# Expert stage of a convolution, attention and mixture-of-experts kernel: expert groups issued interleaved with four weight slots, output written two images at a time

## Chip, cores and metric

The kernel runs on one core of a Trainium2 chip (trn2). The metric is the device time of one execution in microseconds (us), lower is better. A comparison is made over several runs, by their median.

## What is computed

The input is four images of 128 channels by 64 by 64 pixels. Layer 0 adds a deformable 3x3 convolution, layer 1 adds an attention block and then a layer of 64 experts with top-8 routing over the tokens of each image. The change touches the last of these only, which the reference writes so (x is the token tensor, 4 x 4096 x 128, after a layer norm):

```
logits = jnp.einsum('bsd,ed->bse', x, gate_w) + gate_b
probs = jax.nn.softmax(logits, axis=1)
vals, idx = jax.lax.top_k(probs.transpose(0, 2, 1), K)
...
pooled = jnp.einsum('bked,bke->bed', gathered, topv)
h = jax.nn.gelu(jnp.einsum('ebd,edh->ebh', h, weight1), approximate=False)
out = jnp.einsum('ebh,eho->ebo', h, weight2)
weighted = jnp.einsum('beo,bke->bkeo', out, topv).reshape(Bn, K * E, O)
outputs = outputs.at[jnp.arange(Bn)[:, None], flat_idx].add(weighted)
```

The result is `t + outputs`, turned back to channels by pixels. Biases stand as an extra row of `weight1` and `weight2`. All of it is f32.

## The kernel before, in words

The program is a chain of stages with a barrier between them: offsets, first convolution, the main stage (attention with the convolution and the feed-forward of other images beside it), a last feed-forward round, and `stage_experts`. The first four are the same on both sides. All instructions are written out by hand for each engine, and the order on an engine is the order of the code; semaphores tie the engines together.

`stage_experts` has three parts, in this order:

- **Routing**, two images at a time (a duo). Tokens are loaded to `xn`, normalised on ACT, turned on PE by transposes (L1640), multiplied with the gate (L1650); DVE picks the top 8 and makes `sel[duo]`, a 128 x 4096 matrix whose rows 0 to 63 are the experts of the duo's first image and rows 64 to 127 those of its second. `sel` is turned (L1656) and pools the tokens (L1665) into `pooled`.
- **Experts**, 16 groups of four. For a group, `weights` on SP (L1504, L1506) issues five DMAs, 2 MB in all, into one of `SLOTS` = 2 slots, as soon as the product that read the slot before is done (`o_full`). PE multiplies the four experts' pooled vectors (4 columns each, put at column tiles 0, 32, 64, 96) with the first weights (L1679, `eps_h`), ACT copies the result (L1625), PE turns it (L1683), DVE adds the bias (L1571), ACT applies Gelu (L1627), PE does 16 products with the second weights (L1688, `eps_o`), DVE copies (L1573), PE turns it (L1692), DVE adds the second bias (L1576). Only then does PE start the next group: nothing of group g+1 overlaps group g but its weights' loading. The code is a loop whose body has two groups.
- **Output**, 32 steps, one chunk of 512 tokens of one image each. PE makes the chunk's expert sum, a product over the 64 rows of that image in `sel` (L1704), and adds the tokens themselves by four products of a token tile with the identity into the same PSUM bank (L1706). DVE copies the bank to `y` (L1584), SP stores it (L1491). Two banks and two `y` buffers alternate. The tokens are loaded again from memory, 2 MB an image, the first two images after all weights, the others during the output (L1519).

Of the kernel before, what the change touches and what calls it, by code (L numbers as in the profile page):

```python
# [10 lines left out]
ALU = mybir.AluOpType  # L11
# [3 lines left out]
P = 128  # L15
# [1425 lines left out]
SLOTS = 2  # L1441


def stage_experts(nc, d, ident, stack):
# [18 lines left out]
    pooled, pooled_g = sb("pooled", [P, NEXP, IMAGES]), [sb(f"pooled_g{i}", [P, EXPERTS_AT_ONCE, IMAGES]) for i in range(SLOTS)]  # L1463

    hs = [sb(f"hs{i}", [P, 512]) for i in range(SLOTS)]
    hb = [sb(f"hb{i}", [P, 4, EXPERTS_AT_ONCE, IMAGES]) for i in range(SLOTS)]
    hg = [sb(f"hg{i}", [P, 4, EXPERTS_AT_ONCE, IMAGES]) for i in range(SLOTS)]
    os = [sb(f"os{i}", [P, P]) for i in range(SLOTS)]
    out_t, out_e = sb("out_t", [P, IMAGES, NEXP]), [sb(f"out_e{i}", [P, P]) for i in range(DUOS)]
    y = [sb(f"y{i}", [P, 512]) for i in range(2)]  # L1470
# [3 lines left out]
     dv, bias_full, bias_done, pg_ready, h_full, hs_ready, ht_full, hb_ready, hg_ready, o_full, os_ready, ot_full, o_done, oe_full,  # L1474
     oe_done, y_full, y_free, cleared, ln_ready) = (
        sem(n) for n in ("e_consts", "e_biases", "e_tr_full", "e_tr_free", "lg_full", "lg_free", "xn_ready", "ex_ready", "s_ready",
                         "st_full", "pool_full", "pool_free", "top_ready", "e_dve", "bias_full", "bias_done", "pg_ready", "h_full",
                         "hs_ready", "ht_full", "hb_ready", "hg_ready", "o_full", "os_ready", "ot_full", "o_done", "oe_full",
                         "oe_done", "y_full", "y_free", "e_cleared", "ln_ready"))
    x_in = [sem(f"e_x_in{i}") for i in range(2)]  # L1480
    w_in = [sem(f"w_in{i}") for i in range(SLOTS)]
    y_out = [sem(f"y_out{i}") for i in range(2)]
# [4 lines left out]

    def stores(sp, b):
        for c in range(CHUNKS):
            sp.wait_ge(y_free, b * CHUNKS + c + 1)  # L1490
            sp.dma_start(d.out[b, :, c * 512:(c + 1) * 512], y[c % 2][:]).then_inc(y_out[c % 2], 16)  # L1491

    @block.sync
    def _(sp):
# [18 lines left out]
        with sp.Fori(1, NG // SLOTS) as i:  # L1513
            for s in range(SLOTS):
                sp.wait_ge(o_full, (i - 1) * SLOTS + s + 1)
                weights(i * SLOTS + s, s)
        for b in range(IMAGES):
            sp.wait_ge(pool_full, IMAGES) if b < 2 else sp.wait_ge(y_full, (b - 1) * CHUNKS)
            sp.dma_start(xn[b % 2][:], tokens(b)).then_inc(x_in[b % 2], 16)  # L1519
            if b:  # L1520
                stores(sp, b - 1)
        stores(sp, IMAGES - 1)
        for i in range(2):
            sp.wait_ge(y_out[i], IMAGES * CHUNKS // 2 * 16)

    @block.vector
    def _(dve):
# [36 lines left out]
        with dve.Fori(0, NG // SLOTS) as i:  # L1564
            for s in range(SLOTS):
                g = i * SLOTS + s
                es = bass.ds(g * EXPERTS_AT_ONCE, EXPERTS_AT_ONCE)
                v.tensor_copy(pooled_g[s][:], pooled[:, es, :]).then_inc(pg_ready, 1)
                dve.wait_ge(ht_full, g + 1)
                bias1 = b1_t[:, :, es].rearrange("p c (e o) -> p c e o", o=1).to_broadcast([P, 4, EXPERTS_AT_ONCE, IMAGES])  # L1570
                v.tensor_tensor(hb[s][:], ps_t[0][:].rearrange("p (c e b) -> p c e b", c=4, b=32)[:, :, :, 0:IMAGES], bias1, ALU.add).then_inc(hb_ready, 1)  # L1571
                dve.wait_ge(o_full, g + 1)
                v.tensor_copy(os[s][:], ps_o[:, 0:P]).then_inc(os_ready, 1)  # L1573
                dve.wait_ge(ot_full, g + 1)
                bias2 = b2_t[:, es].rearrange("p (o e) -> p o e", o=1).to_broadcast([P, IMAGES, EXPERTS_AT_ONCE])
                v.tensor_tensor(out_t[:, :, es], ps_t[1][:, 0:P].rearrange("p (e b) -> p b e", b=32)[:, 0:IMAGES, :], bias2, ALU.add).then_inc(o_done, 1)  # L1576
# [3 lines left out]
        for n in range(IMAGES * CHUNKS):  # L1580
            dve.wait_ge(y_full, n + 1)
            if n >= 2:
                dve.wait_ge(y_out[n % 2], n // 2 * 16)
# [248 lines left out]
```

## Time and profile before

| | |
|---|---|
| median of 3 runs | 8955.63 us (8911.77, 8955.63, 8959.74) |
| profiled execution: its own time | 8972.61 us |
| profiled execution: span of the trace | 8970.8 us |
| PE, ACT, DVE, POOL busy | 7595.3, 7673.2, 3781.7, 1154.8 us |
| mean granted TensorE clock | 0.936 |
| expert groups (8714.4 to 8838.1) | 123.7 us |
| output steps (8839.2 to 8967.5) | 128.3 us |

The trace is of one execution. Times in it are counted from the start of the span. PE is the matrix engine (PEld its weight loads), ACT, DVE, POOL and SP are the other engines; SPq rows are DMAs that SP issues. A granted clock of 1.00 is 2.4 GHz, 0.50 is 1.2 GHz. A product of f32 operands shows as two records of PE, a transpose as one. "DMA share" is the mean busy share of the core's 16 DMA engines; since it counts the time of packets that overlap in an engine, it can be somewhat over 1.

### The profile page before, as it was taken

The numbers are of one execution on the slowest core, as the hardware profiler recorded it, in microseconds if no ns is written. First come the engines' busy times: TensorE is split into PE (matmuls) and PEld (weight loads), VectorE is DVE, ScalarE is ACT, GpSimd is POOL, SyncE is SP. The second block draws the span as 40 slices with busy tenths as digits, with TensorE's granted clock in tenths as the row PEclk, the third lists the DMA queues.
The fourth block names the chain that finished last, engine by engine and source line by source line (L and its number), as shares of the span: only waits on it lengthen the run. The fifth ranks groups of instructions, "written<-read, shape, count | busy, mean of one in ns | idle before, by whom it ended". The sixth has DMA issues, their size and how long they took to land. (4 is left out here: it accounts for less than half of the span.)

```text
span 8970.8 us, 172356 instructions
## 1 busy us (share of the span) xinstructions
PE 7595.3 (85%) x59323; PEld 2167.8 (24%) x59323; DVE 3781.7 (42%) x14439; ACT 7673.2 (86%) x6204; POOL 1154.8 (13%) x1165
## 2 busy tenths in 40 slices
PE   4354989999999999999999999999988888888558
PEld 1343222222222222222222222222222121212134
DVE  4566333333334555454555454544533222224421
ACT  1222999999999999999999999999999999998541
POOL 0553111111111111111111111111000000000000
PEclk8676999999999999999999999999999999999775
DMA  6553111111111111111111111111100000000115
GB/s 211 165 150 99 49 48 50 47 49 48 49 48 49 51 50 50 48 52 52 51 50 50 49 52 45 50 53 51 31 11 7 8 8 8 7 8 13 52 49 176
DMA packets 514912, 491.53 MB, mean 55 GB/s; under 512 B 228057, under 2 KB 417177, under 8 KB 513570
## 3 DMA queue, kind: packets, MB, share of 16 engines
q0 software_dynamic: 92880, 304.42, 11.7%
q1 hardware_dynamic: 421202, 176.26, 7.5%
q8 instruction: 494, 8.09, 0.4%
q14 instruction: 336, 2.75, 0.1%
HBM read 398.77 MB, written 81.79 MB: 54 GB/s over the span
## 5 line engine op out<-in xcount | busy, mean ns | idle before, releaser
L921 ACT ACTIVATE e<-sc 128x1536 f32<-128x1536 f32 x5376 | 7281.0, 1678 | 182.8 <-PE sc L852 176.6
L871 PE MATMUL acc<-e,v_cur 128*9 128x512 f32 x32256 | 4333.9, 602 | 9.8 <-DVE acc_sb L803 9.8
L852 PE MATMUL sc<-b_unit,a_cur 32*128 32x512 f16 x16384 | 2184.2, 388 | 627.6 <-ACT e L921 567.8
L852 PEld LDWEIGHTS sc<-b_unit,a_cur 32*128 32x128 f16 x16384 | 538.7, 91 | 4560.6 <-ACT e L921 4148.9
L553 POOL DMA_INDIRECT corners<-table,idx_st x873 | 867.6, 994 | 4754.8 <-ACT e L921 4657.9
L871 PEld LDWEIGHTS acc<-e,v_cur 128*9 128x9 f32 x32256 | 485.9, 88 | 965.2 <-issue 953.8
L577 DVE SCALAR_TENSOR_TENSOR val<-corners,w_st,val 128x128 f32<-128x128 f32 x2619 | 711.5, 346 | 1.8
L803 DVE COPY acc_sb<-acc 128x512 f32<-128x512 f32 x129 | 89.2, 692 | 1371.5 <-PE acc L871 1350.4
L500 PE MATMUL cf_ps_t<-ident,cf_val 128*128 128x128 f32 x1152 | 172.9, 311 | 271.4 <-DVE cf_val L421 154.0
L475 ACT COPY cf_val_t<-cf_ps_t 128x512 f32<-128x512 f32 (+1 forms) x96 | 44.0, 479 | 404.1 <-PE cf_ps_t L500 266.8
L382 POOL DMA_INDIRECT cf_corners<-table,cf_idx x288 | 287.0, 997 | 473.3 <-DVE cf_idx L407 236.1
L591 DVE COPY val_t<-misc 128x512 f32<-128x512 f32 (+1 forms) x288 | 160.8, 558 | 433.4 <-PE misc L624 432.3
L632 PE MATMUL misc<-dcnw,val_t 128*128 128x128 f32 x1728 | 243.8, 286 | 0.0
L500 PEld LDWEIGHTS cf_ps_t<-ident,cf_val 128*128 128x128 f32 x1152 | 163.0, 225 | 279.6 <-issue 278.3
L632 PEld LDWEIGHTS misc<-dcnw,val_t 128*128 128x128 f32 x1728 | 207.3, 191 | 43.5 <-issue 43.5
L814 DVE RECIPROCAL rs<-misc 128x16 f32<-128x16 f32 x129 | 33.1, 256 | 392.4 <-PE misc L825 392.0
L754 DVE COPY a_next<-misc 128x1024 f16<-128x1024 f16 (+1 forms) x64 | 44.3, 692 | 354.4 <-PE misc L766 349.0
L600 DVE TENSOR_TENSOR t_out<-misc,xt 128x128 f32<-128x128 f32 x96 | 28.0, 292 | 379.6 <-PE misc L632 379.6
L575 DVE TENSOR_SCALAR val<-corners,w_st 128x128 f32<-128x128 f32 x873 | 180.1, 282 | 12.4 <-DVE ctx_t L816 12.1
L421 DVE SCALAR_TENSOR_TENSOR cf_val<-cf_corners,cf_w,cf_val 128x128 f32<-128x128 f32 x576 | 157.5, 346 | 43.4 <-remote 35.5
L921 ACT ACTIVATE e_tail<-sc 128x1024 f32<-128x1024 f32 x128 | 173.6, 1356 | 0.0
L1017 DVE TENSOR_SCALAR val_t<-misc 128x512 f32<-128x512 f32 x96 | 66.4, 692 | 254.1 <-PE misc L1052 254.1
(326 smaller groups left out, 4854.9 us busy)
## 6 DMA issues: line engine op xcount, KB each, us to landing
table<-pix SPq DMA_DIRECT2D x16, 2304.0 KB, 18.4
ew<-in_ew SPq DMA_DIRECT2D x16, 1024.0 KB, 5.4
ew<-in_ew SPq DMA_DIRECT2D x64, 256.0 KB, 6.1
corners<-table,idx_st POOLq DMA_INDIRECT x873
x_ch<-in_x SPq DMA_DIRECT2D x4, 2048.0 KB, 10.8
qn<-q SPq DMA_DIRECT2D x64, 128.0 KB
ctx<-ctx_t SPq DMA_DIRECT2D x128, 64.0 KB, 1.8
out<-y SPq DMA_DIRECT2D x32, 256.0 KB, 2.0
```

Of the source, the lines that this page charges most:

```text
L382: pool.indirect_dma_start(corners[j][:, k, :], None, d.table, bass.IndirectOffsetOnAxis(idx_st[j][:, k:k + 1], 0)).then_inc(gathered[j], 16)
L421: last = v.scalar_tensor_tensor(out=dst, in0=src, scalar=wt, in1=dst, op0=ALU.mult, op1=ALU.add)
L500: last = nc.tensor.matmul(ps_t[at % 2][:, (k - g0) * P:(k - g0 + 1) * P], val[j % 2][c][:, k, :], r.ident[:], start=(c == 0), stop=(c == 1))
L553: pool.indirect_dma_start(self.corners[s][:, k, :], None, self.d.table, bass.IndirectOffsetOnAxis(self.idx_st[s][:, k:k + 1], 0)).then_inc ...
L575: last = v.tensor_scalar(val[:, k, :], src, wt, None, ALU.mult)
L577: last = v.scalar_tensor_tensor(out=val[:, k, :], in0=src, scalar=wt, in1=val[:, k, :], op0=ALU.mult, op1=ALU.add)
L591: m.dve_give(v.tensor_copy(self.val_t[:, g0 * P:g1 * P], m.bank[:, 0:(g1 - g0) * P]))
L632: last = self.nc.tensor.matmul(m.bank[:, 0:P], self.val_t[:, k * P:(k + 1) * P], self.r.dcnw[:, k, :], start=(k == 0), stop=(k == TAPS - 1))
L803: self.nc.vector.tensor_copy(self.acc_sb[:], self.acc[:]).then_inc(self.acc_read, 1)
L852: last = self.nc.tensor.matmul(self.sc[k % self.SC][:, i, :], self.a[rows, t * P:(t + 1) * P], self.bst[u % 2][rows, :], start=True, stop= ...
L871: last = self.nc.tensor.matmul(self.acc[32 * h:32 * h + self.E1, :], self.v[:, t, h, :], self.e_of(j)[:, i, :], start=(t == 0), stop=(t == ...
L921: self.nc.scalar.activation(self.e_of(j)[:], self.sc[k % self.SC][:, 0:width, :], ACT.Exp, scale=1.0 / HD ** 0.5).then_inc(self.exp_done, 1)
```

## The change

- **Four weight slots** in place of two; the slots of `hs`, `hb`, `hg`, `os` stay two. `pooled_g`, a copy of four experts' columns, goes away, and PE reads `pooled` itself.
- **Groups are interleaved.** The loops are written out. PE's order for step g is: turn of the hidden values of g, hidden product of g+1, turn of the outcome of g-1, outcome product of g. DVE takes over the copy of the hidden product from ACT (`copy_h`), so ACT does only Gelu.
- **The tokens are loaded again between the weights**: image 0 before the weights of group 4, then one image before those of groups 7, 10 and 13, into four places (`raw`) that are free by then. After the last weights SP has only stores left.
- **Output in 16 steps of two images.** Each step handles the same chunk of both images of a duo: two products over 64 rows each (rows 0 to 63 and rows 64 to 127) into two banks (`sums`), then eight transposes of token tiles into two further banks (`turns`). ACT copies the turned tokens to `y`, which now lies in `xn_t`, DVE adds the sum from PSUM in place, SP stores two pieces of 256 KB.

```diff
-SLOTS = 2
+SLOTS = 4
...
-    y = [sb(f"y{i}", [P, 512]) for i in range(2)]
+    y = [[xn_t[:, (2 * j + i) * 512:(2 * j + i + 1) * 512] for i in range(2)] for j in range(2)]
...
+    raw = [xn[0][:], xn[1][:], big[:].rearrange("p (t c) -> p t c", c=P), s_t[:]]
+    sums = ((ps_l[0], ps_l[1]), (ps_h, ps_o))
+    turns = ((ps_t[0], ps_t[1]), (ps_p, ps_b))
...
+        sp.wait_ge(pool_full, IMAGES)
+        sp.wait_ge(s_ready, DUOS)
+        for g in range(SLOTS, NG):
+            if (g - SLOTS) % 3 == 0:
+                b = (g - SLOTS) // 3
+                sp.dma_start(raw[b], tokens(b)).then_inc(again[b], 16)
+            sp.wait_ge(o_full, g - SLOTS + 1)
+            weights(g, g % SLOTS)
+        for step in range(STEPS_OUT):
+            duo, c = divmod(step, CHUNKS)
+            for i in range(2):
+                sp.wait_ge(y_free, 2 * step + i + 1)
+                sp.dma_start(d.out[2 * duo + i, :, c * 512:(c + 1) * 512], y[c % 2][i]).then_inc(y_out[c % 2][i], 16)
...
+        copy_h(0)
+        for g in range(NG):
+            add_b1(g)
+            if g + 1 < NG:
+                copy_h(g + 1)
+            if g:
+                add_b2(g - 1)
+            copy_o(g)
+        add_b2(NG - 1)
...
+        for step in range(STEPS_OUT):
+            at = step % 2
+            dve.wait_ge(y_full, step + 1)
+            for i in range(2):
+                dve.wait_ge(turned, 2 * step + i + 1)
+                v.tensor_tensor(y[at][i], y[at][i], sums[at][i][:], ALU.add).then_inc(y_free, 1)
...
+        for step in range(STEPS_OUT):
+            at = step % 2
+            act.wait_ge(y_full, step + 1)
+            for i in range(2):
+                if step >= 2:
+                    act.wait_ge(y_out[at][i], step // 2 * 16)
+                nc.scalar.copy(y[at][i], turns[at][i][:]).then_inc(turned, 1)
...
+        hidden(0)
+        for g in range(NG):
+            turn_hidden(g)
+            if g + 1 < NG:
+                hidden(g + 1)
+            if g:
+                turn_outcome(g - 1)
+            outcome(g)
+        turn_outcome(NG - 1)
...
-                T.matmul(ps_l[c % 2][:], out_e[b // 2][half, :], sel[b // 2][half, c * 512:(c + 1) * 512], start=True, stop=False)
+            if step >= 2:
+                pe.wait_ge(y_free, 2 * (step - 1))
+            for i in range(2):
+                half = slice(NEXP * i, NEXP * (i + 1))
+                T.matmul(sums[at][i][:], out_e[duo][half, :], sel[duo][half, c * 512:(c + 1) * 512], start=True, stop=True)
+            for i in range(2):
                 for j in range(4):
-                    last = T.matmul(ps_l[c % 2][:, j * P:(j + 1) * P], xn[b % 2][:, 4 * c + j, :], ident[:], start=False, stop=(j == 3))
+                    last = T.transpose(turns[at][i][:, j * P:(j + 1) * P], raw[2 * duo + i][:, 4 * c + j, :], ident[:])
+            last.then_inc(y_full, 1)
```

The order of PE in the expert part. The engine is PE, the place is the loop body before (two groups; `eps_h` is the hidden product, `eps_t<-ident,hs` its turn, `eps_o` the outcome, `eps_t<-ident,os` its turn):

```order
L1679 MATMUL eps_h<-ew_0,pooled_g 4x512 [waits hs_ready,pg_ready]
L1679 MATMUL eps_h<-ew_0,pooled_g 4x512 x3
L1683 MATMUL eps_t<-ident,hs 128x128 [waits hs_ready]
L1683 MATMUL eps_t<-ident,hs 128x128 x3
L1688 MATMUL eps_o<-ew_0,hg 4x128 [waits hg_ready]
L1688 MATMUL eps_o<-ew_0,hg 4x128 x15
L1692 MATMUL eps_t<-ident,os 128x128 [waits o_done,os_ready]
L1676 REGISTER_ALU [waits w_in1]
L1679 MATMUL eps_h<-ew_1,pooled_g 4x512 [waits hs_ready,pg_ready]
```

and the same engine in the change, at the last groups:

```order
L1711 MATMUL eps_h<-ew_3,pooled 4x512 [waits w_in3]
L1711 MATMUL eps_h<-ew_3,pooled 4x512 x3
L1732 MATMUL eps_t<-ident,os 128x128 [waits o_done,os_ready]
L1726 MATMUL eps_o<-ew_2,hg 4x128 [waits hg_ready]
L1726 MATMUL eps_o<-ew_2,hg 4x128 x15
L1718 MATMUL eps_t<-ident,hs 128x128 [waits hb_ready,hs_ready]
L1718 MATMUL eps_t<-ident,hs 128x128 x3
L1732 MATMUL eps_t<-ident,os 128x128 [waits o_done,os_ready]
L1726 MATMUL eps_o<-ew_3,hg 4x128 [waits hg_ready]
L1726 MATMUL eps_o<-ew_3,hg 4x128 x15
L1732 MATMUL eps_t<-ident,os 128x128 [waits o_done,os_ready]
```

The hidden product of group 15 (slot 3), which waits for the last weights, now stands ahead of the outcome of group 14.

The queue of DMAs that SP issues, in the change, from the end of routing (before, the loads of tokens `xn_tok<-t` stood behind the last `ew`):

```order
L1518 DMA xn_tok<-t 128x32x128 [waits s_ready,pool_full]
L1504 DMA ew_0<-in_ew 128x4x512 [waits o_full]
L1506 DMA ew_0<-in_ew 128x4x128 x4
L1504 DMA ew_1<-in_ew 128x4x512 [waits o_full]
L1506 DMA ew_1<-in_ew 128x4x128 x4
L1504 DMA ew_2<-in_ew 128x4x512 [waits o_full]
L1506 DMA ew_2<-in_ew 128x4x128 x4
L1518 DMA xn_tok<-t 128x32x128
L1504 DMA ew_3<-in_ew 128x4x512 [waits o_full]
```

The tokens of image 0 moved ahead of the weights of group 4, and those of image 1 ahead of group 7's.

PE in the output, before:

```order
L1704 MATMUL eps_l<-selected,out_e 128x512 [waits y_free]
L1706 MATMUL eps_l<-ident,xn_tok 128x128 x4
L1704 MATMUL eps_l<-selected,out_e 128x512 [waits y_free]
L1706 MATMUL eps_l<-ident,xn_tok 128x128 x4
L1704 MATMUL eps_l<-selected,out_e 128x512 [waits y_free]
```

and now:

```order
L1757 MATMUL eps_l<-selected,out_e 128x512 [waits e_again1,e_again0,oe_done]
L1757 MATMUL eps_l<-selected,out_e 128x512
L1760 MATMUL eps_t<-ident,xn_tok 128x128 x8
L1757 MATMUL eps_h<-selected,out_e 128x512
L1757 MATMUL eps_o<-selected,out_e 128x512
L1760 MATMUL eps_p<-ident,xn_tok 128x128 x4
L1760 MATMUL eps_b<-ident,xn_tok 128x128 x4
L1757 MATMUL eps_l<-selected,out_e 128x512 [waits y_free]
```

Two products stand next to each other where one stood, and the eight token tiles are transposes (one record each) where they were products (two records each).

## Rows read from the trace of the kernel before

**Rows 1.** The page, busy time by engine.

```profile
PE 7595.3 (85%) x59323; PEld 2167.8 (24%) x59323; DVE 3781.7 (42%) x14439; ACT 7673.2 (86%) x6204; POOL 1154.8 (13%) x1165
```

**Rows 2.** Stretches: length, busy PE, PEld, DVE, ACT, POOL; clock, DMA share, GB/s.

```profile
8714.40:8838.10 123.70, 82.78 (x720) 32.08 (x720) 13.69 (x64) 32.71 (x47) 0.00 (x0) 0.54 0.91 259
8839.20:8967.50 128.30, 128.26 (x320) 72.90 (x320) 21.44 (x31) 0.00 (x0) 0.00 (x0) 0.50 0.32 106
```

**Rows 3.** Timeline of one expert group: start, us, engine, line, operation.

```profile
8752.69 1.89 PE L1679 MATMUL eps_h<-ew,pooled_g 128*4 128x512 f32 x8 [0.51 <-DVE pooled_g L1568]
8754.65 0.58 ACT L1625 COPY hs<-eps_h 128x512 f32<-128x512 f32 x1 [5.30 <-PE eps_h L1679]
...
8755.29 1.11 PE L1683 MATMUL eps_t<-ident,hs 128*128 128x128 f32 x4 [0.71 <-ACT hs L1625]
...
8757.10 1.89 PE L1688 MATMUL eps_o<-ew,hg 128*4 128x128 f32 x32 [0.69 <-ACT hg L1627]
...
8759.40 0.48 PE L1692 MATMUL eps_t<-ident,os 128*128 128x128 f32 x1 [0.41 <-DVE os L1573]
...
8760.01 0.18 DVE L1576 TENSOR_TENSOR out_t<-eps_t,b_t 128x16 f32 x1 [0.67 <-PE eps_t L1692]
```

**Rows 4.** Timeline of SP's queue: first reload of weights, reload of tokens.

```profile
8720.24 0.38 SPq L1504 DMA_DIRECT2D ew<-in_ew  x1
...
8824.87 8.92 SPq L1519 DMA_DIRECT2D xn_tok<-t  x2
```

**Rows 5.** Stretches, columns as in rows 2: the transfers.

```profile
8736.00:8826.00 90.00, 60.84 (x506) 22.98 (x507) 9.75 (x46) 24.47 (x35) 0.00 (x0) 0.52 0.94 269
8490.00:8510.00 20.00, 0.00 (x0) 0.00 (x0) 11.23 (x79) 0.27 (x1) 0.00 (x0) 0.50 1.05 298
...
8850.00:8860.00 10.00, 10.00 (x28) 6.09 (x27) 2.00 (x3) 0.00 (x0) 0.00 (x0) 0.50 0.13 52
```

**Rows 6.** Timeline: the last group's first product, the first of the output.

```profile
8830.62 1.89 PE L1679 MATMUL eps_h<-ew,pooled_g 128*4 128x512 f32 x8 [0.52 <-DVE pooled_g L1568]
...
8839.24 2.07 PE L1704 MATMUL eps_l<-selected,out_e 64*128 64x512 f32 x2 [0.38 <-DVE out_e L1579]
```

**Rows 7.** Groups of the output by shape: operation, count, busy, mean ns, idle before.

```profile
L1706 PE MATMUL eps_l<-ident,xn_tok 128*128 128x128 f32 x256 | 66.4, 441 | 0.0
L1704 PE MATMUL eps_l<-selected,out_e 64*128 64x512 f32 x64 | 66.3, 1138 | 0.4 <-DVE out_e L1579 0.4
...
L1584 DVE COPY y<-eps_l 128x512 f32<-128x512 f32 x32 | 22.1, 692 | 106.9 <-PE eps_l L1706 102.4 <-DMA out<-y 4.6
```

**Rows 8.** Timeline of output steps.

```profile
8849.25 2.07 PE L1706 MATMUL eps_l<-ident,xn_tok 128*128 128x128 f32 x8
8851.26 2.07 PE L1704 MATMUL eps_l<-selected,out_e 64*128 64x512 f32 x2
```

**Rows 9.** Products over 32 rows in the main stage: the page's group.

```profile
L852 PE MATMUL sc<-b_unit,a_cur 32*128 32x512 f16 x16384 | 2184.2, 388 | 627.6 <-ACT e L921 567.8
```

**Rows 10.** Timeline of the main stage: three of them together.

```profile
4000.66 0.39 PE L852 MATMUL sc<-b_unit,a_cur 32*128 32x512 f16 x3
```

**Rows 11.** Transposes of the routing: timeline, and durations min/median/max in ns.

```profile
8522.20 6.15 PE L1640 MATMUL eps_t<-ident,xn_tok 128*128 128x128 f32 x32 [46.47 <-ACT xn_tok L1593]
```

```profile
L1640 PE MATMUL eps_t<-ident,xn_tok x128: 272/273/477, 8522.2 to 8663.3; 128*128 128x128 f32 x128
```

**Rows 12.** Stretches, columns as in rows 2: where those transposes run, and output steps.

```profile
8521.90:8525.30 3.40, 3.10 (x14) 2.74 (x15) 0.00 (x0) 1.57 (x4) 0.00 (x0) 0.50 0.00 0
8525.30:8528.70 3.40, 3.21 (x21) 2.02 (x20) 0.00 (x0) 3.07 (x6) 0.00 (x0) 1.00 0.00 0
8840.00:8900.00 60.00, 60.00 (x151) 34.17 (x150) 10.24 (x15) 0.00 (x0) 0.00 (x0) 0.50 0.35 114
```

**Rows 13.** The end: last copy, and the stores' time to landing.

```profile
8967.56 0.69 DVE L1584 COPY y<-eps_l 128x512 f32<-128x512 f32 x1 [3.31 <-PE eps_l L1706]
```

```profile
DMA to landing us min/median/max: 2.0/2.0/8.4
```

More of the change, by code:

```diff
@@ L1512, in _ @@
             sp.dma_start(xn[b % 2][:], tokens(b)).then_inc(x_in[b % 2], 16)
[L1513 to L1524, printed above, removed]
+        sp.wait_ge(pool_full, IMAGES)
[11 more added lines that the diff above has]
+                sp.dma_start(d.out[2 * duo + i, :, c * 512:(c + 1) * 512], y[c % 2][i]).then_inc(y_out[c % 2][i], 16)
+        for j in range(2):
+            for i in range(2):
+                sp.wait_ge(y_out[j][i], STEPS_OUT // 2 * 16)
     @block.vector
@@ L1563, in _, with copy_h @@
         dve.wait_ge(bias_done, 2)
[L1564 to L1576, printed above, removed]
+        def copy_h(g):
+            dve.wait_ge(h_full, g + 1)
+            if g >= 2:
+                dve.wait_ge(ht_full, g - 1)
+            v.tensor_copy(hs[g % 2][:], ps_h[:]).then_inc(hs_ready, 1)
@@ new lines, in hidden, with turn_hidden @@
+        def hidden(g):
+            s = g % SLOTS
+            pe.wait_ge(w_in[s], (g // SLOTS + 1) * 16 * (1 + EXPERTS_AT_ONCE))
+            for e in range(EXPERTS_AT_ONCE):
+                last = T.matmul(ps_h[32 * e:32 * e + IMAGES, :], pooled[:, g * EXPERTS_AT_ONCE + e, :], w1[s][:, e, :], start=True, stop=True)
+            last.then_inc(h_full, 1)
+        def turn_hidden(g):
+            pe.wait_ge(hs_ready, g + 1)
+            pe.wait_ge(hb_ready, g)
+            for c in range(4):
+                last = T.transpose(ps_t[0][:, c * P:(c + 1) * P], hs[g % 2][:, c * P:(c + 1) * P], ident[:])
+            last.then_inc(ht_full, 1)
@@ new lines, in outcome, with turn_outcome @@
+        def outcome(g):
+            s = g % SLOTS
+            pe.wait_ge(hg_ready, g + 1)
+            for c in range(4):
+                for e in range(EXPERTS_AT_ONCE):
+                    last = T.matmul(ps_o[32 * e:32 * e + IMAGES, 0:P], hg[g % 2][:, c, e, :], w2[s][:, e, c, :], start=(c == 0), stop=(c == 3))
+            last.then_inc(o_full, 1)
+        def turn_outcome(g):
+            pe.wait_ge(os_ready, g + 1)
+            pe.wait_ge(o_done, g)
+            T.transpose(ps_t[1][:, 0:P], os[g % 2][:], ident[:]).then_inc(ot_full, 1)
```

94 lines of the change are left out of this document (41 added, 53 removed).

## Prediction

> **What bounds the kernel now.** I read the page's busy times first, then the stretches of the expert stage, then timelines inside them. PE and ACT are busy for 85% and 86% of the span [rows 1], but that is the main stage, which the change leaves alone. What counts is the last 256 us, where the stretches show two parts [rows 2]. In the expert groups (123.7 us for 16, so 7.7 us each) PE is busy for 82.8 us only, and the DMA engines at a share of 0.91. In the output (128.3 us for 32 steps) PE is busy all the time, at a granted clock of 0.50, which is 1.2 GHz, with DMA at 0.32. So the output is bound by PE at its low clock. The groups are bound twice, closely: by a serial chain and, nearly, by the transfers.
>
> The chain is seen in one group's timeline [rows 3]: product 1.89, copy on ACT 0.58, turn 1.11, then 0.7 us for bias and Gelu (8756.40 to 8757.10), product 1.89, copy and turn, second bias done at 8760.19. PE works 1.89 + 1.11 + 1.89 + 0.48 = 5.4 us of it. The transfers: in the middle of the part, 269 GB/s at a share of 0.94 [rows 5].
>
> **The expert groups after the change.** Interleaved, a group costs PE at least 5.4 us at the low clock, 86 us for 16 groups. But what is transferred between the end of routing (about 8713) and the last group grows. Before, 14 groups of weights (2.097 MB each) were loaded there, from 8720.24 on, and the tokens only from 8824.87 [rows 4]. Now 12 groups and four images of tokens, also 2.097 MB each, are: 16 units, 33.6 MB. At a full share the rate is 269 / 0.94 = 286 GB/s; the deeper queue at the start of the stage gives 298 / 1.05 = 284 [rows 5]. So 117.5 us. The first packets can move at about 8714.5, since the tokens of image 0 are issued as soon as pooling is done, and the weights of group 4 are queued behind them when group 0 frees its slot, so there is no hole. The last weights land at about 8832; before, the last group's product started at 8830.62 [rows 6].
>
> Behind the last weights now stands more than before: hidden product of group 15 (1.9), then, since it was put ahead of them, turn 13 (0.5) and the outcome of 14 (1.9), then turn 15 (1.1), bias and Gelu (0.7), outcome 15 (1.9) and its copy, turn and bias (1.2, 8758.99 to 8760.19) [rows 3]; with 0.5 for the landing about 10 us. The part ends at 8842 where it ended at 8838.1: **+4 us**. The overlap is paid for by the tokens; it does not shorten the part. Bounds: the highest rate seen, 298 GB/s, gives 113 us, thus -1; the mean rate of the whole part before, 259 [rows 2], gives 130 us, thus +16. The stretch at the start of the stage is nearest, since it too has several transfers queued.
>
> Small edits of this part cost nothing: `pooled_g` goes (0.2 us per group, off the path now); the copy on DVE takes 0.69 in place of 0.58 [rows 7, 3] and lies under the outcome product of 1.89. If the transfers were faster than PE, that copy would still be hidden. Loading four slots at the start adds 4.2 MB, 15 us of transfers, early in the stage, when nothing else is loaded before image 2.
>
> **The output, one step.** Before, a step is 128.3 / 32 = 4.0 us: from the token products to the sum's product 2.0 us, and 2.0 us back [rows 2, 8]. In the change a step covers two chunks. Its eight transposes are eight records, as the four token products were: 2.0 us (four take 1.11 us with the last one's run-out [rows 3]). Its two sum products use rows 0 to 63 and rows 64 to 127 of the array. What they cost together no row shows for this shape. From below: as one, 2.0 us. From above: one after the other, 4.0 us. The nearest rows are products over 32 rows, each 388 ns long, of which three end 0.39 us after the first began, so they run side by side [rows 9, 10]; and for f32 the four hidden products on different columns, eight records, take 1.89 us, where two records alone take 2.07 [rows 3, 8]. I take 2.0. A step is then 4.0 us at the low clock, for twice the work: 16 steps, 64 us.
>
> **The clock.** Here I go one step on. All through the output the clock is 0.50 though PE is busy for 60.00 of 60 us [rows 12], and half of that time is a product that uses only 64 of the 128 rows [rows 7]. At the first transposes of the routing, over all 128 rows, 3.10 of 3.40 us busy, the clock was at 0.50 too, and after those 3.4 us it was at 1.00 and stayed there [rows 12]. These were transposes alone [rows 11]. In the changed output both halves of the rows are at work together, then transposes over all of them, so nothing is left that uses half of the array. I expect the clock to rise in the first steps and stay up. The Trainium skill ("TensorE: Matmul & The Clock Gate", Part 4: PE-mode transpose) says the opposite of transposes: the full clock does not engage for them. By it the sum would be -59 us rather than -86; this trace does not agree with it [rows 11, 12].
>
> At the full clock PE's half of a step halves, to 2.0 us. Then the chain counts: PE's last run-out 0.2, two copies on ACT of 0.58, one add on DVE of 0.69 behind the second, and three hand-overs, together 2.3 us, before PE may use the same banks. Two steps then take 2.0 + 2.3 = 4.3, thus 2.2 us each. DVE (1.4) and ACT (1.2) fit. Two stores a step are 524 KB in 2.2 us, 240 GB/s; a stretch of stores alone moved 52 GB/s at a share of 0.13, thus 400 at full share [rows 5], and a store lands 2.0 us after issue [rows 13], before ACT wants its buffer two steps on. With 5 us at the low clock first (1.25 steps): 5 + 14.75 x 2.2 = 37.5 us, against 128.3: **-91 us**. Bounds: 34 (2.0 a step) and 64 (low clock). If the store becomes late, ACT is next, at some 3 us a step.
>
> **The end.** Before, one copy on DVE (0.69) and a store follow the last product [rows 13]; now two copies on ACT and the add: **+1 us**.
>
> **Sum:** +4 - 91 + 1 = -86 us, against the profiled execution's own 8972.61 (span 8970.8), thus 8887. That execution is 17 us above the median of the runs, 8955.63, so I predict 8955.6 - 86 = 8870 us.
>
> **Rivals.** All against the median.
> - *The clock stays low.* For it: 128 us of busy PE at 0.50 [rows 2]. Against it: the rise after transposes [rows 12]. The output takes 64 us: +4 - 64 + 1 = -59, thus 8897. The page of the Trainium skill named above would have it so.
> - *The two sum products run one after the other.* They are f32 products of two records each, and no row shows such a pair on different rows. A step is then 6 us, and since half the rows idle again, the clock stays low: 96 us, +4 - 32 + 1 = -27, thus 8929.
> - *ACT, DVE and the stores set the pace* at 3 us a step: 5 + 14.75 x 3 = 49 us, +4 - 79 + 1 = -74, thus 8882.
> - *Slower than before: the transfers choke.* Tokens and weights in one long queue, with the last weights behind all of it. It decides once the rate falls below 33.6 MB / (117.5 + 86) = 165 GB/s. At 150 GB/s the transfers take 224 us in place of 117.5: +4 + 106 - 91 + 1 = +20, thus 8976; over 0.5% slower needs some 135 GB/s. Against it: 298 GB/s with as many transfers queued [rows 5].
> - *The overlap does nothing* is not a rival but part of the forecast.
>
> **How the numbers follow.** The forecast has a chance of 0.62, the low clock 0.16, the pair in turn 0.11, the pace of the copies 0.08, the choked transfers 0.03. The runs of one kernel lie between 8912 and 8960, and one profile at 8973, so the level itself may move. The range goes from the forecast on the lowest of those levels, 8912 - 86 = 8826, to the low clock on the highest, 8897 + 17 = 8914, rounded to 8825 and 8915; it leaves out the pair in turn and the choke, 0.14. About 0.5%, 45 us, is what a measurement can tell from no change. Over it lie the forecast, the low clock and the pace of the copies, 0.86, less a little since 59 is close to 45: faster 0.84. Same 0.13, slower 0.03.
>
> **What would show it.** Expert groups: DMA share near 1 from 8714 on, PE waiting for `ew` from about group 7 on, the part ending within a few us of 8842. Output: the pair of sum products as four records in 2.1 us or less, not 4; 16 steps; clock 1.00 from the second or third step; steps of 2.0 to 2.3 us; ACT's waits on `out<-y` small. Wrong if the clock stays at 0.50, if the sum products stand in a row, or if the last weights land after 8845.

## The result and the profile after

| | before | after |
|---|---|---|
| median (4 runs each, taken together) | 8948.38 us (8911.77 to 8959.74) | 8840.6 us (8838.6 to 8852.54) |
| ratio, 95% interval | | 0.989 [0.9873, 0.9906] |
| profiled execution: own time, span | 8972.61, 8970.8 | 8852.54, 8850.7 |
| end of routing (last copy of `pooled`) | 8713.3 | 8696.7 |
| expert part, from there to the last `out_t` | 124.8 | 113.4 |
| gap to the first sum product | 1.1 | 1.0 |
| output, from there to the end of the span | 131.5 | 39.7 |
| **from the end of routing to the end** | 257.5 | 154.1 |

The forecast was 8870 in a range of 8825 to 8915; the median is 8840.6. The spans differ by 120.1 us. Of that, 16.6 lie ahead of the end of routing. They lie ahead of the expert stage too: its first load is issued at 8487.1 before and at 8469.7 after, and from there to the end of routing it is 226.2 and 227.0 us, so the two more slots that are loaded there cost less than 1 us. Over the 13 profiled kernels of this study the end of routing lies anywhere from 8673 to 8718, which is variation between executions. The change itself is the last line, **-103.4 us**, where the forecast's sum was -86. All experiments are judged by that line. It comes from one execution of each kernel, but parts that two kernels have in common agree closely in it: the expert part of after, e2, e3 and e7 takes 113.4 to 113.6 us, the output of after, e5, e6, e8 and e9 39.6 to 39.9. The medians stand beside it; they carry the variation ahead of the stage.

The page of after, busy time by engine, beside [rows 1]:

```profile
PE 7470.6 (84%) x59195; PEld 2103.8 (24%) x59195; DVE 3787.0 (43%) x14439; ACT 7662.5 (87%) x6205; POOL 1126.8 (13%) x1165
```

PE loses 125 us of busy time, more than the span does. The stretches of after: the expert part, the output, the output's inner steps, and the middle of the expert part (length, busy PE, PEld, DVE, ACT, POOL; clock, DMA share, GB/s), beside [rows 2, 5]:

```profile
8696.40:8810.10 113.70, 61.69 (x725) 26.93 (x725) 21.57 (x67) 4.10 (x16) 0.00 (x0) 0.74 1.02 296
8810.10:8850.70 40.60, 34.30 (x194) 18.74 (x194) 21.05 (x34) 17.36 (x32) 0.00 (x0) 0.99 0.56 207
8811.00:8846.00 35.00, 33.74 (x192) 18.54 (x192) 19.24 (x31) 16.29 (x30) 0.00 (x0) 1.00 0.57 210
8706.00:8800.00 94.00, 46.33 (x499) 19.08 (x495) 14.18 (x44) 2.82 (x11) 0.00 (x0) 0.70 1.11 323
```

Three things are to be seen. The output runs at a clock of 1.00 where it ran at 0.50. PE is busy for only 54% of the expert part, so something else sets its length. And the DMA engines move 323 GB/s at a share of 1.11, while the forecast took 286 GB/s, the rate at a share of 1.00, for full.

The output in detail, from the timeline of after (start, us, engine, line, operation), beside [rows 8]:

```profile
8819.50 1.13 PE L1757 MATMUL eps_l<-selected,out_e 64*128 64x512 f32 x4
8819.56 0.58 ACT L1661 COPY xn_ch<-eps_p 128x512 f32<-128x512 f32 x1 [1.01 <-PE eps_b L1760]
...
8820.24 0.69 DVE L1612 TENSOR_TENSOR xn_ch<-xn_ch,eps_h 128x512 f32<-128x512 f32 x1 [0.80 <-ACT xn_ch L1661]
8820.56 1.09 PE L1760 MATMUL eps_t<-ident,xn_tok 128*128 128x128 f32 x8
...
8821.59 0.69 PE L1757 MATMUL eps_h<-selected,out_e 64*128 64x512 f32 x1
...
8821.59 0.69 PE L1757 MATMUL eps_o<-selected,out_e 64*128 64x512 f32 x1
...
8823.72 1.13 PE L1757 MATMUL eps_l<-selected,out_e 64*128 64x512 f32 x4
```

Two records of different banks (`eps_h`, `eps_o`) begin at the same time and take 0.69 us: the pair on rows 0 to 63 and 64 to 127 does run side by side. All four records of a pair take 1.13 us. Two steps take 8823.72 - 8819.50 = 4.22 us, 2.11 each.

What the expert part waits for, from the waits of 8700 to 8851 (engine, line, what it waited for: us in total, times, longest):

```profile
ACT hg L1654 <- DVE hb L1581: 121.5, 16, 18.0
...
PE eps_h L1711 <- DMA ew<-in_ew: 49.3, 12, 9.2
...
DVE xn_ch L1612 <- ACT xn_ch L1661: 16.6, 16, 2.9
```

ACT's 121.5 us are those of an engine with nothing else to do. PE waits for weights at each of the 12 loaded groups, 49.3 us in all: the part is bound by transfers. The last group, beside [rows 6]:

```profile
8804.61 1.04 PE L1711 MATMUL eps_h<-ew,pooled 128*4 128x512 f32 x8 [1.66 <-DMA ew<-in_ew]
...
8809.92 0.17 DVE L1593 TENSOR_TENSOR out_t<-eps_t,b_t 128x16 f32<-128x16 f32 x1 [0.42 <-PE eps_t L1732]
...
8811.07 1.13 PE L1757 MATMUL eps_l<-selected,out_e 64*128 64x512 f32 x4 [0.47 <-DVE out_e L1606]
```

The hidden product took 1.04 us, at the full clock, where it took 1.89 before [rows 6]; and the tail behind the last weights is 8810.1 - 8804.6 = 5.5 us. The granted clock is 1.00 from 8802.38 on, so the output inherits it from the last expert groups. How they came to raise it is not isolated by any run. It is not the length of the part: with two slots (e5, below) the part is 195.7 us long, and the output starts at 1.00 all the same.

### The profile page after: what moved, and what is told of

The parts are those of the page before. It is cut to its first block and busy times, and to the rows that moved or that the text cites. A ratio compares the mean times of both kernels' runs of the same rounds, so it can differ in the third digit from the quotient of the medians.

```text
span 8850.7 us, 171835 instructions
## 1 busy us (share of the span) xinstructions
PE 7470.6 (84%) x59195; PEld 2103.8 (24%) x59195; DVE 3787.0 (43%) x14439; ACT 7662.5 (87%) x6205; POOL 1126.8 (13%) x1165
## 5 line engine op out<-in xcount | busy, mean ns | idle before, releaser
L553 POOL DMA_INDIRECT corners<-table,idx_st x873 | 839.9, 962 | 4778.7 <-ACT e L921 4682.0
L803 DVE COPY acc_sb<-acc 128x512 f32<-128x512 f32 x129 | 89.2, 692 | 1369.8 <-PE acc L871 1350.3
L575 DVE TENSOR_SCALAR val<-corners,w_st 128x128 f32<-128x128 f32 x873 | 179.9, 281 | 12.5 <-DVE ctx_t L816 12.5
```

The lines of the kernel that those rows point to most:

```text
L553: pool.indirect_dma_start(self.corners[s][:, k, :], None, self.d.table, bass.IndirectOffsetOnAxis(self.idx_st[s][:, k:k + 1], 0)).then_inc ...
L575: last = v.tensor_scalar(val[:, k, :], src, wt, None, ALU.mult)
L803: self.nc.vector.tensor_copy(self.acc_sb[:], self.acc[:]).then_inc(self.acc_read, 1)
```

## The experiments

Edits are against the changed kernel unless said. In the table, part, output and total are the stretches of the table above in one profiled execution (the total has the gap between part and output in it); the median and ratio are against the kernel before, measured beside it.

| run | what differs | part | output | total | median | ratio, 95% |
|---|---|---|---|---|---|---|
| before | | 124.8 | 131.5 | 257.5 | 8948 to 8958 | |
| after | | 113.4 | 39.7 | 154.1 | 8840.6 | 0.989 [0.9873, 0.9906] |
| e1_out_only | groups of before, output of after | 121.2 | 51.0 | 179.5 | 8858.6 | 0.9907 [0.9887, 0.9927] |
| e2_groups_only | groups of after, output of before | 113.5 | 130.3 | 244.7 | 8935.0 | 0.9973 [0.9954, 0.9992] |
| e3_split_pair | the pair taken apart | 113.4 | 100.7 | 215.1 | 8897.8 | 0.9942 [0.9925, 0.9958] |
| e4_full_rows | before, sum product over 128 rows | 125.6 | 80.2 | 207.7 | 8883.6 | 0.9924 [0.9905, 0.9943] |
| e5_two_slots | two slots | 195.7 | 39.6 | 236.3 | 8934.1 | 0.9975 [0.9958, 0.9992] |
| e6_in_series | four slots, groups in series | 116.6 | 39.7 | 157.3 | 8867.0 | 0.9888 [0.9859, 0.9916] |
| e7_by_products | products in place of transposes | 113.6 | 53.3 | 167.9 | 8864.4 | 0.9894 [0.9877, 0.991] |
| e8_long_rows | second weights in 2 KB pieces | 104.3 | 39.6 | 144.9 | 8832.5 | 0.9861 [0.9843, 0.9879] |
| e9_three_slots | three slots | 125.8 | 39.9 | 166.7 | 8866.5 | 0.9895 [0.9861, 0.9929] |
| e10_late_tokens | two images' tokens after the weights | 101.3 | 41.6 | 143.8 | 8850.3 | 0.9882 [0.9853, 0.9911] |
| e11_long_late | e8 and e10 together | 89.2 | 40.3 | 130.5 | 8821.6 | 0.9857 [0.9828, 0.9885] |

### Which half does it, and what raises the clock

**e1_out_only** takes the groups back to the order and the two slots of before, with the copy of the hidden product on ACT again, and puts all tokens after the weights. The loops stay written out, and PE reads `pooled` itself.

```diff
-SLOTS = 4
+SLOTS = 2
...
-            if (g - SLOTS) % 3 == 0:
-                b = (g - SLOTS) // 3
-                sp.dma_start(raw[b], tokens(b)).then_inc(again[b], 16)
             sp.wait_ge(o_full, g - SLOTS + 1)
             weights(g, g % SLOTS)
+        for b in range(IMAGES):
+            sp.dma_start(raw[b], tokens(b)).then_inc(again[b], 16)
...
         for g in range(NG):
+            hidden(g)
             turn_hidden(g)
-            if g + 1 < NG:
-                hidden(g + 1)
-            if g:
-                turn_outcome(g - 1)
             outcome(g)
+            turn_outcome(g)
```

> The new output with the groups as they were before (in series, two slots, tokens loaded after the last weights). Theory A, two images at once put all 128 rows to work and that raises the clock: the output starts at 0.50, as the groups end at 0.50, and goes to 1.00 within 5 us; the 16 steps take 37 us, the kernel about 90 us less than before, 8858. Theory B, the clock was high in the changed kernel only because the groups handed it over high: it stays at 0.50, the 16 steps take 64 us, the kernel 63 less than before, 8885.

**e2_groups_only** is the other half: 32 output steps of one image, as before.

```diff
-                T.matmul(sums[at][i][:], out_e[duo][half, :], sel[duo][half, c * 512:(c + 1) * 512], start=True, stop=True)
+                T.matmul(ps_l[c % 2][:], out_e[b // 2][half, :], sel[b // 2][half, c * 512:(c + 1) * 512], start=True, stop=False)
...
-                    last = T.transpose(turns[at][i][:, j * P:(j + 1) * P], raw[2 * duo + i][:, 4 * c + j, :], ident[:])
+                    last = T.matmul(ps_l[c % 2][:, j * P:(j + 1) * P], raw[b][:, 4 * c + j, :], ident[:], start=False, stop=(j == 3))
```

> The new groups, slots and loads with the output as it was before (32 steps, products over 64 rows, tokens by products with the identity). The groups take 114 us, 11 less than before, in either theory, and hand over the clock at 1.00. Theory A with a strict reading (half the rows idle lets the clock fall): the output is back at 0.50 and 128 us, the kernel 11 under before, 8937. Theory B, the clock once up stays up under a busy PE: 32 steps at 2.05 us, 66 us, the kernel 73 under before, 8875.

**e3_split_pair** keeps everything but the pair: each sum product is followed by its own four transposes.

```diff
                 T.matmul(sums[at][i][:], out_e[duo][half, :], sel[duo][half, c * 512:(c + 1) * 512], start=True, stop=True)
-            for i in range(2):
                 for j in range(4):
```

> The changed kernel with the two sum products of a step pulled apart: product and four transposes of one image, then of the other. If the pair runs side by side in the changed kernel, a step gets longer by one product at the full clock, 0.9 to 1.1 us: 16 steps take 50 us in place of 35, the kernel 8856. If standing together is worth nothing: no change, 8841. If half-used rows also lose the clock: 96 us for the steps, 8902.

**e4_full_rows** is the kernel before with one edit: `out_e` has a tile for each image whose other 64 rows are zero, and the sum product goes over all 128 rows.

```diff
-                T.matmul(ps_l[c % 2][:], out_e[b // 2][half, :], sel[b // 2][half, c * 512:(c + 1) * 512], start=True, stop=False)
+                T.matmul(ps_l[c % 2][:], out_e[b][:], sel[b // 2][:, c * 512:(c + 1) * 512], start=True, stop=False)
```

> The kernel before, with one edit: the sum product of each image runs over all 128 rows, the expert values of the other image's 64 rows set to zero, so PE does as many steps of the same length on the same order. Theory A: the clock rises within 5 us of the output's start and stays, the 32 steps take about 70 us in place of 128, the kernel 58 under before, 8890. Theory B: nothing in the output itself raises it, it stays at 0.50, no change, 8948.

Stretches of e1: the wait ahead of the output with its first product, the output's first steps, the next ones:

```profile
8794.20:8801.20 7.00, 0.55 (x2) 0.15 (x2) 0.51 (x2) 0.00 (x0) 0.00 (x0) 0.50 1.06 290
8801.20:8805.70 4.50, 4.45 (x14) 2.60 (x16) 0.00 (x0) 0.44 (x1) 0.00 (x0) 0.50 1.06 291
8805.80:8815.90 10.10, 6.01 (x36) 3.18 (x32) 2.57 (x4) 1.61 (x4) 0.00 (x0) 1.00 1.05 304
```

Here the rise can be seen that the forecast spoke of: the output begins at 0.50, and after 4.5 us of pairs and transposes the clock is 1.00. Stretches of e2, at the first products and then to the end:

```profile
8807.60:8810.00 2.40, 2.39 (x9) 1.64 (x10) 0.00 (x0) 0.00 (x0) 0.00 (x0) 0.80 0.03 7
8810.00:8934.00 124.00, 124.00 (x311) 70.42 (x310) 21.44 (x31) 0.00 (x0) 0.00 (x0) 0.50 0.17 66
```

The expert groups handed over a full clock, and in this execution the steps of before lost it within 2 us and did not have it again, with PE busy for every one of 124 us. Splitting the pair does the same (e3, output), and filling the rows undoes it (e4, its first steps, and the steps up to a stall):

```profile
8807.50:8898.00 90.50, 90.49 (x181) 36.31 (x182) 18.00 (x28) 15.48 (x29) 0.00 (x0) 0.51 0.22 82
```

```profile
8808.40:8813.80 5.40, 5.33 (x13) 3.27 (x14) 0.71 (x2) 0.00 (x0) 0.00 (x0) 0.50 0.76 207
8813.90:8837.70 23.80, 18.49 (x109) 13.52 (x107) 6.23 (x9) 0.00 (x0) 0.00 (x0) 1.00 0.59 198
```

e4 adds no useful work, only zeros on the idle half of the rows, and takes 51 us off the output. So what holds the clock down in these profiled executions is the product over 64 of 128 rows when it is alone, and what raises it is all rows at work, be it by a pair or by zeros. In e3, one image's half step takes 3.05 us (the timeline of its PE):

```profile
8851.74 2.07 PE L1757 MATMUL eps_o<-selected,out_e 64*128 64x512 f32 x2
8853.75 1.11 PE L1759 MATMUL eps_b<-ident,xn_tok 128*128 128x128 f32 x4
8854.79 2.07 PE L1757 MATMUL eps_l<-selected,out_e 64*128 64x512 f32 x2
```

That is 6.1 us for two images, the 6 us of the rival "the pair in turn"; its output of 100.7 us is that rival's 96 and its end. The two halves of the change, from 257.5: the output alone gives -78.0, the groups alone -12.8, together they give -103.4. The 12.6 us between come from e1's end: its gap and output are 17.5 us longer than those of after (51.0 + 7.2 against 39.7 + 1.0), of which 4.8 are covered, since its part is 3.6 shorter than that of before and the output of e2 1.2 shorter. PE waits for tokens first, and then stores stand in the queue behind the tokens of images 2 and 3. The waits of e1:

```profile
ACT xn_ch L1659 <- DMA out<-xn_ch: 10.7, 3, 8.4
...
PE eps_l L1751 <- DMA xn_tok<-t: 6.5, 1, 6.5
```

In e4, whose tokens of images 2 and 3 are loaded during the output too, the same thing costs more (DVE's waits):

```profile
DVE y L1587 <- DMA out<-y: 18.8, 3, 8.3
```

Two of e2's ten runs took 8876.1 and 8890.1 at a mean clock of 0.947 and 0.946, where its profiled run had 0.940. The faster one is at what the expectation gives for a clock that stays up through the whole output (8875). The level ahead of the stage does not explain it: with e2's 244.7 us behind it, the end of routing would lie at 8630, 43 us earlier than in any of the 13 profiles. So it seems that a full clock, once handed over, can also be kept by steps with half-filled rows. Neither execution was profiled; this is an inference, and what decides between the two courses is open.

**e7_by_products** takes the transposes away and keeps the pair.

```diff
-                    last = T.transpose(turns[at][i][:, j * P:(j + 1) * P], raw[2 * duo + i][:, 4 * c + j, :], ident[:])
+                    last = T.matmul(turns[at][i][:, j * P:(j + 1) * P], raw[2 * duo + i][:, 4 * c + j, :], ident[:], start=True, stop=True)
```

> The changed kernel with the tokens turned by f32 products with the identity (two records each) in place of transposes (one each). If PE sets the step: 8 records more at 0.11 us at the full clock, 0.9 us a step, 14 us in all, 8855. If the copies on ACT and DVE set it: no change, 8841. The clock stays at 1.00 in either case.

Its output, and its eight token products in the timeline:

```profile
8810.40:8856.00 45.60, 45.59 (x300) 32.43 (x300) 18.00 (x28) 15.03 (x28) 0.00 (x0) 1.00 0.42 156
```

```profile
8817.56 2.05 PE L1760 MATMUL eps_t<-ident,xn_tok 128*128 128x128 f32 x16
```

PE is busy all the time, at 1.00: 16 records take 2.05 us where 8 transposes took 1.09. The output is longer by 13.6 us for 16 steps, 0.85 each; the transposes give that and nothing else. The clock is full with them and without them. The Trainium skill ("TensorE: Matmul & The Clock Gate", Part 4: PE-mode transpose) has it, from another kernel, that transposes do not engage the full clock. Here transposes alone went from 0.50 to 1.00 [rows 11, 12], and in after, steps of which half are transposes keep 1.00 for 35 us, so the measurement decides against that sentence here.

### What shortens the expert part

**e6_in_series** keeps the four slots and the tokens between the weights, but runs group after group, on PE as shown and on DVE in the same way.

```diff
         for g in range(NG):
+            hidden(g)
             turn_hidden(g)
-            if g + 1 < NG:
-                hidden(g + 1)
-            if g:
-                turn_outcome(g - 1)
             outcome(g)
+            turn_outcome(g)
```

> The changed kernel with four slots and tokens between the weights, but each group after the other on PE as before. Theory A, the interleaving is what lets the part follow the transfers: PE's series of 7.7 us a group decides, the part takes 125 us in place of 114 and hands the clock over low, which costs the output 2 to 3 us: 8855. Theory B, the transfers decide in either order and only the last group is slower, by 2 us: 8843.

**e5_two_slots** and **e9_three_slots** keep the interleaved order and change the number of slots (`SLOTS = 2`, `SLOTS = 3`), with one condition more so that still just four images of tokens are loaded.

> The changed kernel with two weight slots in place of four, interleaved groups and tokens between the weights kept; 14 groups of weights and 4 images are then loaded in the part, 18 units in place of 16. Theory A, the rate of 317 GB/s comes of the deeper queue that four slots allow: it falls to about 280, the part takes 135 + 8 = 143 us in place of 114, the kernel 8870. Theory B, the rate belongs to the mix of transfers and the written-out code: 317 stays, the part takes 119 + 8 = 127 us, the kernel 8854.

> The changed kernel with three weight slots, interleaved groups and tokens between the weights kept; 13 groups and 4 images in the part, 17 units. From the end of pooling to the end of the kernel the changed kernel takes 154.1 us. Theory A, the stall of two slots comes of the order (the load into a slot waits for a product that stands behind the next group's weights), and three slots leave two loads outstanding, enough to keep the DMA engines full: 35.7 MB at 320 GB/s, the part 120 us in place of 113.4, 161 in all, the kernel 8848. Theory B, the rate grows with the queue's depth and three slots give 285 GB/s: the part 133 us, 174 in all, 8861.

The middle of e6's part, and its waits for weights:

```profile
8712.00:8810.00 98.00, 56.96 (x594) 22.94 (x594) 18.17 (x53) 3.33 (x13) 0.00 (x0) 0.67 1.10 320
```

```profile
PE eps_h L1707 <- DMA ew<-in_ew: 17.2, 4, 8.6
```

With the groups in series the DMA engines still move 320 GB/s, and PE still waits for weights; the part is 3.2 us longer, 116.6, which is what the theory that transfers decide gives (116; the chain theory gave 125). So with four slots **interleaving is worth 3 us**. The rest is there without it: e6 is 8.2 us below the part of before, although 16 units of 2.097 MB (12 groups and four images) are loaded in it where 14 were. Of these 8.2 us, 3.6 come with e1 already (121.2), which has two slots and the groups in series as well; what is left to explain them are the written-out loops and PE's reading of `pooled` itself. Against e1, e6 has the two slots more, the tokens in between and the copy on DVE, and needs 4.6 us less for two units more. The median of e6, 8867.0, lies over both theories (8843 and 8855) and does not decide between them; the part and the total (157.3) do. With two slots it is the other way round, and neither theory had foreseen the size. The timeline of e5, two groups:

```profile
8740.27 0.37 SPq L1504 DMA_DIRECT2D ew<-in_ew  x1
...
8748.98 1.89 PE L1711 MATMUL eps_h<-ew,pooled 128*4 128x512 f32 x8 [7.73 <-DMA ew<-in_ew]
...
8751.21 1.51 PE L1726 MATMUL eps_o<-ew,hg 128*4 128x128 f32 x32
8752.79 0.37 SPq L1504 DMA_DIRECT2D ew<-in_ew  x1
...
8761.52 1.89 PE L1711 MATMUL eps_h<-ew,pooled 128*4 128x512 f32 x8 [8.21 <-DMA ew<-in_ew]
```

In the interleaved order the outcome of g stands behind the hidden product of g+1. The slot of g is free only after that outcome, and g+1 has the other slot: when the load for g+2 is issued, the one for g+1 has just been used, and no other weights are on their way. Each load of weights runs by itself, 8.7 us from issue (8740.27) to use (8748.98), then 3.8 us of PE work, and again: 12.5 us a group. PE waits for weights 14 times, 117.5 us in all, and the part moves 193 GB/s on average. More slots are not a bonus to the interleaved order, they are its condition. Three give 125.8 us, between the 120 and the 133 of the two theories and no better than the kernel before, though with 17 units in place of 14; the rate in the middle of its part is between the others too:

```profile
8708.00:8825.00 117.00, 60.57 (x659) 26.20 (x662) 19.17 (x58) 3.58 (x14) 0.00 (x0) 0.73 1.03 299
```

**e8_long_rows** changes how the second weights, half of a load's bytes, are cut: partition p takes rows 4p to 4p+3, which lie together in memory as 2 KB, in place of rows p, p+128, p+256, p+384 of 512 B each. The turn of the hidden values takes every fourth column to match.

```diff
-                sp.dma_start(w2[s][:, x], d.ew2[bass.ds(g * EXPERTS_AT_ONCE + x, 1), 0:512, :].rearrange("o (c p) h -> p (o c) h", p=P)).then_inc(w_in[s], 16)
+                sp.dma_start(w2[s][:, x], d.ew2[bass.ds(g * EXPERTS_AT_ONCE + x, 1), 0:512, :].rearrange("o (p c) h -> p (o c) h", p=P)).then_inc(w_in[s], 16)
...
-                last = T.transpose(ps_t[0][:, c * P:(c + 1) * P], hs[g % 2][:, c * P:(c + 1) * P], ident[:])
+                last = T.transpose(ps_t[0][:, c * P:(c + 1) * P], hs[g % 2][:].rearrange("p (q c) -> p c q", c=4)[:, c, :], ident[:])
```

> The changed kernel with the second weights laid out so that each partition reads 2 KB in one piece in place of four pieces of 512 bytes (partition p takes hidden rows 4p to 4p+3, and the turn of the hidden values takes every fourth column). If the short pieces cost what their packets show, 32 ns for 512 bytes against 97 for 2 KB, the 12 groups loaded in the part need 8 to 11 us less, the part takes 104 us in place of 114, the kernel 8831. If the rate has a common limit whatever the pieces are: no change, 8841.

The middle of its part:

```profile
8688.00:8775.00 87.00, 49.83 (x581) 22.73 (x577) 16.75 (x52) 3.07 (x12) 0.00 (x0) 0.74 1.05 361
```

361 GB/s in place of 323, and a part shorter by 9.1 us, with nothing changed but the pieces and the turn that goes with them. The first weights lay in pieces of 2 KB all along. With the two kinds of pieces apart it is plainer still. The first line is a stretch of e8 in which weights alone move, all in 2 KB pieces; the second is one of e10 (below) in which tokens alone move, in rows of 512 B:

```profile
8759.00:8773.00 14.00, 6.43 (x58) 2.31 (x62) 1.43 (x5) 0.26 (x1) 0.00 (x0) 0.63 1.05 386
```

```profile
8811.40:8823.00 11.60, 9.86 (x89) 4.50 (x90) 2.40 (x9) 0.26 (x1) 0.00 (x0) 0.65 1.06 291
```

The engines are as full in both, and the rate is 386 and 291 GB/s. From these two rates the bytes of the part can be priced, as an estimate: in after 12.6 MB in long pieces and 21.0 MB in short ones, 32.6 + 72.1 = 105 us, where 106.1 were measured; in e8 25.2 and 8.4 MB, 65.2 + 28.8 = 94 us, 11 less, where the part became 9.1 shorter. The Trainium skill ("DMA: Bandwidth & Descriptors", Specifications) gives 512 B as the least transfer that reaches line rate. Here pieces of 512 B do not reach it: in the trace of after a packet of 512 B takes 32 ns on its engine, so four take 128 ns, and one of 2 KB of weights takes 88 ns in e8.

**e10_late_tokens** leaves only images 0 and 1 between the weights and loads images 2 and 3 after the last weights, ahead of the stores. **e11_long_late** is that and e8.

```diff
-            if (g - SLOTS) % 3 == 0:
+            if (g - SLOTS) % 3 == 0 and g < SLOTS + 6:
...
             weights(g, g % SLOTS)
+        for b in range(2, IMAGES):
+            sp.dma_start(raw[b], tokens(b)).then_inc(again[b], 16)
```

> The changed kernel with the tokens of images 2 and 3 loaded behind the last weights, those of images 0 and 1 as they are. Theory A, the part lasts as long as what is queued ahead of the last weights: two units less, 13 us, the part 100 us; the loads then stand before the first stores and hold ACT's copies up for about 4 us: 145 in all in place of 154.1, the kernel 8832. Theory B, PE would decide (16 groups at 5.4 us at the low clock and the start, 90 us) or the stores' delay eats it all: 154.

> Both edits together: second weights in pieces of 2 KB, and the tokens of images 2 and 3 behind the last weights. If transfers still decide: 29.4 MB at 361 GB/s, the part 92 us or a little less, the output 4 us longer than in the changed kernel, 137 in all in place of 154.1, the kernel 8824. If PE decides by now, the part is 90 us and DMA shows gaps: still about 137.

Stretches of e11, the part and the output:

```profile
8673.20:8762.40 89.20, 59.26 (x724) 27.72 (x723) 21.27 (x67) 4.10 (x16) 0.00 (x0) 0.81 1.03 356
8763.40:8803.70 40.30, 33.83 (x192) 18.49 (x192) 20.52 (x32) 17.46 (x32) 0.00 (x0) 0.99 0.71 250
```

Two images fewer ahead of the last weights take 12.1 us off the part (e10), and the output, where the DMA engines had room at a share of 0.56, pays 1.9. Most of that is the clock and not the transfers: in e10 the clock was at 1.00 when the output began, but it fell in the first pair, for 3.5 us, and the pair and its transposes took 1.93 us each in place of 1.13 and 1.09:

```profile
8820.50:8824.00 3.50, 3.50 (x12) 1.76 (x12) 0.00 (x0) 0.00 (x0) 0.00 (x0) 0.51 1.03 291
```

The medians do not show e10's gain over after (8850.3 against 8840.6; ratios 0.9882 and 0.989 to kernels before measured beside them): its profiled execution came to the end of routing at 8718, 21 us later than that of after. Together with the long pieces the total is 130.5 us, 23.6 less than after, at a median of 8821.6: this version beats both kernels. By the ratios alone the step beyond after is less sure: the intervals of the two, against the kernel before, overlap a little ([0.9828, 0.9885] and [0.9873, 0.9906]). PE still waits for weights, 27.2 us in 12 waits:

```profile
PE eps_h L1713 <- DMA ew<-in_ew: 27.2, 12, 7.3
```

## Why the prediction was right, and where it was off

- **The output, -90 with the end: right, -91.8 measured.** The pair runs side by side, four records in 1.13 us at the full clock (2.0 had been taken at the low one); a step takes 2.11 us where 2.2 was forecast; ACT waits for stores 2.5 us in all. At the low clock the pair takes 1.93 us (e10's first), so the 2.0 for it was right too, though no row had shown it. PE is busy for 33.7 of 35 us, so PE and the chain of copies end nearly level, as in the forecast's 4.0 of 4.3. e3 is the rival "the pair in turn" made real, and e7 prices the transposes.
- **The clock: right in its cause, off in its place.** It was to rise in the first steps, with 5 us at the low level. In after it was at 1.00 before the output began, which the forecast had not foreseen and which spared it the 5 us at the low level, some 2.5 us. That part of the gain is luck: the forecast says nothing of the clock at the end of the expert part. e1 shows the rise as forecast, 4.5 us. The reason given, that nothing is left that uses half of the array, is what e4 isolates: rows filled with zeros raise it as well. The inference from transposes alone [rows 11, 12] led there; the rival in which the clock stays low gave 8897. That half-filled rows lose a full clock every time is not shown (e2's two fast executions).
- **The expert part, +4: wrong, -11.4 measured.** The step that failed is the rate, "At a full share the rate is 269 / 0.94 = 286 GB/s". Measured: 33.55 MB from 8698.0 to 8804.1, 106.1 us, 316 GB/s; 117.5 us had been forecast, so 11.4 us of the miss are here. The rate per share did hold for this mix of loads: 323 / 1.11 = 291 GB/s, against 286. What failed is that a share of 1.00 was taken for full, though [rows 5] has one of 1.05; with 1.11 the same sum gives 318. The forecast also gave all bytes one rate, and in the kernel before there were gaps between loads, and two kinds of pieces. In slices of 4 us both show, the first two in the expert part, the third where tokens alone are loaded:

```profile
8808.00:8812.00 4.00, 2.60 (x20) 0.97 (x16) 0.23 (x1) 2.12 (x3) 0.00 (x0) 0.50 1.10 365
8812.00:8816.00 4.00, 3.07 (x41) 1.03 (x29) 0.62 (x3) 0.00 (x0) 0.00 (x0) 0.50 0.79 161
8838.00:8842.00 4.00, 3.45 (x7) 1.55 (x8) 0.62 (x3) 0.00 (x0) 0.00 (x0) 0.50 1.05 290
```

  365 GB/s is a slice that begins with a load in 2 KB pieces, so it is no rate for the whole either; the estimate by pieces under e8 gives 105 us. The bound from the highest rate seen, 298 GB/s and -1 us, was too near, since 316 were reached.
- **The tail behind the last weights, 10 us: 5.5 measured**, since PE worked it off at the full clock. With the 11.4 us above that makes up the 15 us between +4 and -11.4.
- **"The overlap is paid for by the tokens": right in kind.** Two of the four images cost the 12.1 us that e10 gives back, and e6 shows the interleaving itself at 3 us. What I had not seen is that the slots, which keep the queue full, are the larger gain.
- **The transfers choke** did not happen with four slots. e5 comes near it, 193 GB/s, by a mechanism that was not in the list: too few slots for the order.
- The total came out 17 us lower than the sum (-103.4 against -86), and the median 12 us lower again. Of these 12, 7 are the level the forecast started from: the median before was 8955.6 with three runs and is 8948.4 with four. The other 4 or 5 lie outside the stage or between executions; no profile shows which.

## What to carry to other kernels

Where PE is busy all the time at half clock, look for products that use half of the rows; give the other half work or, failing that, zeros, and price the result at both clocks, since a run can differ. Before interleaving a loop that loads its own operands, count which slot is freed by what in the new order, and add slots before anything else. Read transfer rates for each length of pieces, from stretches in which the queue is full, and do not take a share of 1.00 for full. Ask which transfers really must stand ahead of the last one that the chain waits for.

## What the runs showed that was not expected

- Filling 64 idle rows with zeros took 51 us off an output of 131.5 (e4), by the clock alone.
- A full clock that was handed over was lost within 2 us to steps half of whose time is a product over 64 rows (e2, e3), and was kept by pairs with transposes or products over 128 rows (after, e7). Neither is without exception: two of e2's ten executions were some 50 us faster than the rest, and in e10 the first pair and its transposes ran at 0.50 before the clock rose again.
- Interleaving with two slots made the part 70.9 us longer than the serial loop of before (195.7 against 124.8). The four images in it are 8.4 MB, at 291 GB/s 29 us at most (an estimate); the rest is the waiting.
- The rate rose with the slots at the same pieces, 299, then 323 GB/s in the middle of the part for three and four, and with the pieces at the same slots, 323 to 361. Weights in 2 KB pieces alone move at 386 GB/s, tokens in 512 B rows alone at 291, at the same share.
